# The crossed weights of a two-convolution kernel moved as two transfers, one per convolution

## What is computed

```python
def _L0_conv_ref(x, conv1_w, conv1_b, conv2_w, conv2_b, experts_w1, experts_b1, experts_w2, experts_b2, gate_w, gate_b):
    identity = x
    pooled = x.mean(axis=(-2, -1))
    gate = jax.nn.softmax(pooled @ gate_w.T + gate_b)
    kw1 = jnp.einsum('be,eoihw->boihw', gate, experts_w1) + conv1_w
    kb1 = gate @ experts_b1 + conv1_b
    kw2 = jnp.einsum('be,eoihw->boihw', gate, experts_w2) + conv2_w
    kb2 = gate @ experts_b2 + conv2_b
    out1 = jax.nn.relu(per_sample(x, kw1, kb1))      # 3x3, SAME
    out2 = per_sample(out1, kw2, kb2)                # 3x3, SAME
    return identity + out2
...
x = x + _L0_conv_ref(_gn(x), ...)
```

## Time and profile before

| what | value |
|---|---|
| median of 3 runs | 357.04 us |
| the profiled execution's own time | 357.09 us |
| its span, first to last instruction | 355.1 us |
| mean granted TensorE clock | 0.979 |
| TensorE busy | 308.5 us, 87% |
| VectorE, ScalarE, GpSimd busy | 76%, 72%, 58% |
| DMA traffic | 60.87 MB, mean 171 GB/s |
| SyncE's queue, share of 16 DMA engines | 80.8% |

### The profile page before, as it was taken

The page is one execution under the profiler, slowest core; times in us unless marked ns, Lnnn a source line. Parts: engine busy times, 40 slices in busy tenths (PEclk is TensorE's granted clock), DMA queues, the critical chain, the costliest instruction groups (busy, mean ns, idle before and its releaser), DMA issues.

```text
span 355.1 us, 7776 instructions
## 1 busy us (share of the span) xinstructions
PE 308.5 (87%) x3047; PEld 218.8 (62%) x3047; DVE 269.6 (76%) x571; ACT 254.0 (72%) x294; POOL 204.7 (58%) x240
## 2 busy tenths in 40 slices
PE   1416955499999998999899999999999989999994
PEld 2315743257767686777677677766776867655552
DVE  3699955588969798798879897989697978693432
ACT  1155229896969797898879797979697968866710
POOL 8038607593939485676749493949294947921000
PEclk9999969699999999999999999999999999999999
DMA  8942940599999799979998999999998993665055
GB/s 196 223 76 60 223 95 3 109 201 205 202 207 219 176 213 213 212 169 209 217 210 167 210 208 211 183 209 207 218 185 187 216 217 79 166 141 144 2 134 133
DMA packets 109380, 60.87 MB, mean 171 GB/s; under 512 B 102944, under 2 KB 105248, under 8 KB 109344
## 3 DMA queue, kind: packets, MB, share of 16 engines
q1 hardware_dynamic: 108544, 59.79, 80.8%
q10 hardware_dynamic: 608, 0.59, 0.6%
q0 software_dynamic: 192, 0.01, 0.0%
HBM read 19.47 MB, written 18.87 MB: 108 GB/s over the span
## 4 chain that ended last, share of the span: by engine, by line
PE 66%; DVE 18%; DMA 8%; ACT 3%; issue 3%; SPq 1%; ACTq 0%; DVEq 0%
PE pg L381 63%; DVE mix L649 7%; DMA wts<-wts 7%; DVE a L679 2%; DVE col L658 2%; PE pg L340 2%; DVE stats L607 2%; DMA natural<-in_L_conv_conv_w 1%; DVE wts L665 1%; SPq L297 1%; DVE wts L672 1%; PE pstat L361 1%; ACT xh L496 1%; ACT c L549 1%; ACT a L501 1%
## 5 line engine op out<-in xcount | busy, mean ns | idle before, releaser
L381 PE MATMUL pg<-a,wts 128*64 128x480 f16 (+1 forms) x1440 | 291.9, 363 | 11.5 <-DMA wts<-wts 6.1
L381 PE MATMUL pg<-c,wts 128*64 128x480 f16 (+1 forms) x1440 | 292.4, 367 | 0.0
L381 PEld LDWEIGHTS pg<-c,wts 128*64 128x64 f16 x1440 | 154.3, 110 | 49.4 <-issue 0.9
L381 PEld LDWEIGHTS pg<-a,wts 128*64 128x64 f16 x1440 | 155.0, 110 | 46.6 <-DMA wts<-wts 8.5
L539 ACT ACTIVATE hid<-pg,col 128x480 f32<-128x480 f32 x80 | 52.6, 658 | 45.2 <-PE pg L381 36.7
L869 POOL TENSOR_TENSOR a<-xh,a 128x576 f16<-128x576 f32 x64 | 79.0, 1271 | 4.4 <-issue 2.1
L549 ACT COPY c<-a 64x2352 f32<-64x2352 f32 (+2 forms) x48 | 71.9, 1497 | 2.3 <-DVE a L679 1.9
L850 POOL TENSOR_TENSOR col<-col,minus_half 128x1 f32<-128x1 f32 x16 | 13.8, 860 | 99.5 <-DVE col L622 99.5
L679 DVE TENSOR_TENSOR a<-hid,a 128x480 f16<-128x480 f32 x80 | 53.1, 665 | 22.6 <-ACT a L539 22.4
L649 DVE SCALAR_TENSOR_TENSOR mix<-bank,gate,mix 128x386 f32<-128x386 f32 x96 | 62.9, 655 | 2.4
L883 POOL TENSOR_SCALAR img<-img,col 128x1152 f32<-128x1152 f32 x32 | 64.6, 2025 | 0.1
(11 more groups left out here) (60 smaller groups left out, 140.9 us busy)
## 6 DMA issues: line engine op xcount, KB each, us to landing
c<-a SPq DMA_DIRECT2D x28, 588.0 KB, 6.5
img<-in_x SPq DMA_DIRECT2D x56, 288.0 KB, 7.0
out<-img SPq DMA_DIRECT2D x60, 180.0 KB, 3.1
out<-img SPq DMA_DIRECT2D x60, 108.0 KB, 2.4
wts<-wts SPq DMA_DIRECT2D x28, 96.0 KB, 3.2
c<-a SPq DMA_DIRECT2D x8, 294.0 KB, 5.2
img<-in_x SPq DMA_DIRECT2D x16, 144.0 KB, 5.0
out<-img SPq DMA_DIRECT2D x4, 120.0 KB, 2.1
```

The source lines that it names most:

```text
L381: last = nc.tensor.matmul(pg[g][side * 64:side * 64 + 64, at:at + nb * W].rearrange("p (b w) -> p b w", w=W), wts[s.c % WSETS][kind][:, v, ...
```

## The change

The crossed weights of samples 2 to 15 are moved as four DMAs in place of two, of half the size each: those of the first convolution (v = 0) where both were before, those of the second (v = 1) behind the two halves of the store and in front of the image's crossing. There are two semaphores per place of the ring. Group 0 of the first convolution waits for the first one, group 0 of the second convolution for the second one. For samples 0 and 1 VectorE makes four copies in place of two, those of the first convolution first, each pair with its own semaphore.

```diff
-        w_crossed = [sem(f"w_crossed{i}") for i in range(RING)]
+        w_crossed = [[sem(f"w_crossed{i}_{v}") for v in range(2)] for i in range(RING)]
...
-            def cross_weights(t):
+            def cross_weights(t, v):
 
                 sp.wait_ge(w_ok, t.number + 1)
                 st, cr = wts[t.c % WSETS][STRAIGHT], wts[t.c % WSETS][CROSSED]
                 for a, b in ((0, 1), (1, 0)):
-                    sp.dma_start(halves(cr)[a].rearrange("p v a b -> p (v a b)"),
-                                 halves(st)[b].rearrange("p v a b -> p (v a b)")).then_inc(w_crossed[t.ring], 16)
+                    sp.dma_start(halves(cr)[a][:, v].rearrange("p a b -> p (a b)"),
+                                 halves(st)[b][:, v].rearrange("p a b -> p (a b)")).then_inc(w_crossed[t.ring][v], 16)
...
             def slot(s):
                 run(load, s, 2, 4)
-                run(cross_weights, s, 0, 2)
+                run(cross_weights, s, 0, 2, 0)
                 run(store, s, -2, 0, 0)
                 run(store, s, -2, 0, 1)
+                run(cross_weights, s, 0, 2, 1)
                 run(cross1, s, 1, 2)
...
-                    pe.wait_ge(w_crossed[s.ring], 32 * (s.lap + 1))
+                    pe.wait_ge(w_crossed[s.ring][0], 32 * (s.lap + 1))
...
-                pe.wait_ge(w_crossed[0], 32)
+                pe.wait_ge(w_crossed[0][0], 32)
...
                     pe.wait_ge(rim_ok, s.number + 1)
+                    pe.wait_ge(w_crossed[s.ring][1], 32 * (s.lap + 1))
...
-                for a, b in ((0, 1), (1, 0)):
-                    last = nc.vector.tensor_copy(halves(cr)[a].rearrange("p v a b -> p (v a b)"),
-                                                 halves(st)[b].rearrange("p v a b -> p (v a b)"))
-                last.then_inc(w_crossed[t.ring], 32)
+                for v in range(2):
+                    for a, b in ((0, 1), (1, 0)):
+                        last = nc.vector.tensor_copy(halves(cr)[a][:, v].rearrange("p a b -> p (a b)"),
+                                                     halves(st)[b][:, v].rearrange("p a b -> p (a b)"))
+                    last.then_inc(w_crossed[t.ring][v], 32)
```

## The result

The changed kernel took 364.25 us (median of 4 runs, 362.96 to 368.65) against 357.13 for the kernel before (4 runs, 356.76 to 357.82). The ratio is 1.0185, with a 95% interval of 1.015 to 1.0221: it is slower by 5.4 to 7.9 us. The longest of the four is a slow run, which the ratio leaves out; the other three lie between 362.96 and 364.67 us. Measured a second time beside other kernels, it was 363.5 us and 1.0188 (1.0149 to 1.0227). The forecast was 361.6 us in a range of 357.0 to 364.8.

What follows compares the result with a forecast made beforehand. Bound: a two-sample loop through SyncE's queue, where DMA engines run dry before the crossing's issue and TensorE awaits odd samples' weights. 357.04 + 6 x (1.16 - 0.4) = 361.6 us, range 357.0 to 364.8.

Steps and rivals of the forecast that it cites:

- The bound and the loop: Odd samples' weights queue behind SyncE's crossing and load; the two-sample loop grows from 37.7 to 38.4 us.
- The two issues in front of the crossing: Second half's two DMA issues on SyncE delay the crossing 1.16 us per loop, bounds 0.7 to 1.3.
- The shorter tail: 98 KB less at the end of SyncE's queue lands odd samples' weights 0.4 us sooner, bounds 0 to 0.48.
- The sum: Six waiting odd samples each lose 1.16 - 0.4 = 0.76 us: 4.6 us on top of 357.04.
- The clock: Rival: longer TensorE waits drop its clock to half; one fall makes at least 363 us, six at least 371; chance 0.04.
- Nothing for even samples, statistics and the second convolution: Even samples keep their margin; VectorE's statistics and the second convolution's new wait cost TensorE nothing.
- The beginning: VectorE's halved copies start the first convolution at 32.5, not 33.8; TensorE then waits 5.1 us, not 3.78; no gain.
- "No change, since bytes are conserved": Rival: 0.48 us taken from the queue's tail reappears before the load, issue time is hidden; 357.0 us, chance 0.10.

Runs made afterwards that it cites:

- Half the loads: Kernel before the change, with image loads of samples 6 to 15 moving rows 0 to 11 of 24 alone: 350.89 us, ratio 0.9827.
- One empty issue: Kernel before the change, whole weights in front, plus one DMA of 64 partitions x 8 bytes into scratch between stores and crossing: 360.97 us, ratio 1.0086.
- two at a covered place: Kernel before the change, plus two 8-byte-per-partition scratch DMAs in front of the stores, where SyncE waits for fin_ok: 357.64 us, ratio 1.0019.
- the empty issues: Kernel before the change, whole weights in front, plus two DMAs of 64 partitions x 8 bytes into scratch behind the stores: 370.58 us, ratio 1.0376.

## Why the prediction was right

- **The bound and the loop:** right. The loop of two samples was to be 38.4 us and is 38.3 to 38.7, leaving out the one with the clock's fall. Half the loads remove the waits of samples 5 to 13.
- **The two issues in front of the crossing:** taken as 1.16 us each loop; measured 6.71 / 6 = 1.12. One empty issue costs about half, two at a covered place nothing.
- **The shorter tail:** taken as 0.4 us between 0 and 0.48; measured 1.66 / 6 = 0.28 on average (from 0.69 sooner to 0.15 later in a single loop; 0.28 again in the second profile). The front halves of samples 5 to 13 landed 4.1 to 5.0 us after their issue, with 4.4 forecast. The gain is near the 0.23 of the Trainium skill's formula, which is a fit to DMAs issued by GpSimd. This is one mis-sized term: 0.7 us over the six loops. The straight conversion by the engines' bandwidth was too favourable, though the engines are full.
- **The sum:** 4.6 us forecast for the loops, 5.05 measured. The waits on the weights were to be near 10.7 us and are 9.9, because in front of sample 3 TensorE itself was late.
- **The clock:** the second mis-sized term. I gave a fall a chance of 0.04, on the ground that a wait of 1.58 us leaves the clock and one of 3.78 us doesn't. With waits of 2.1 us it fell once in either profile of the changed kernel. 1.67 us of the 6.8 are its part. The rival's price was about right (1.5 us a fall), its chance far too low: it isn't an alternative to the forecast but comes on top of it. The range left the clock out, and with a fall the result lies only 0.55 us below its upper end; that it lies inside is partly luck. One of the six runs of the second measurement is above it (366.71 us).
- **Nothing for even samples, statistics and the second convolution:** right for the sum. VectorE did wait for the load, 4.4 us in five places, and TensorE didn't see it: the 17.36 us from its start to the next stores stayed. Even samples have less room than I left them: none waited in the first profile, one in the second.
- **The beginning:** right in that it brings nothing, and the wait of 5.23 us looks like the 5.1 forecast; but the start at 33.53 instead of 32.5 shows that the halved copies failed. In this trace TensorE's first matmuls took 0.35 us where they had taken 0.53, which made the wait longer; in the second profile they took 0.53 again, and the wait was 3.50 us. The agreement of that number is luck.
- **"No change, since bytes are conserved":** excluded by the empty issues, which have practically no bytes and the full price.

## What to carry to other kernels

On a queue that is full most of the time, look for the places where it runs dry, and count the issues in front of them: there each one moves everything behind it, here by 0.56 us, although the engines seem to be the limit. A transfer that isn't urgent belongs where the issuing engine waits anyway, not simply behind the urgent ones; the same split cost 6.6 us at the one place and brought 1.3 us at the other. When waits of an engine grow, ask what its clock does at their new length.

## What was not expected of the hardware

- A second hardware queue did not overtake: for 2.0 us after the issue, no packet of it ran while 1133 of the first queue's did (on idle engines its first came after 1.1 to 1.3 us), and the 96 KB landed after 4.3 us, as on the first queue (4.0 to 4.2).
- A small DMA behind a large one can hold the issuing engine: two DMAs of 64 x 768 bytes behind the crossing's took 5.11 us to issue (5.0 to 5.5 in all slots with a load behind them), elsewhere mostly 1.16.
- The clock's fall isn't decided by the length of the wait alone. It fell after waits of 2.12, 2.14, 2.17, 2.20, 2.64 and twice 2.77 us; it stayed after 2.07, 2.10 and, in the run with one empty issue, 2.33 us:

```profile
214.60:218.00 3.40, 3.40 (x37) 2.66 (x37) 2.35 (x6) 1.22 (x2) 0.29 (x1) 1.00 0.97 249
```

- VectorE's copy of 64x384 in float16 takes 0.25 us alone and 1.20 us beside GpSimd, nearly as much as one of 64x768 there (1.3 us).
